# Node degrees from a search in the sorted target list, and a rearranged first third of a graph layer

## The reference

```python
deg = jnp.maximum(jax.ops.segment_sum(jnp.ones(dst.shape), dst, num_segments=6250), 1.0)
xn = _layernorm(x)
f0, f1 = _fctp(x0, x1, W_li0, W_li1, node_attr, MUL)    # f, times 1/sqrt(deg): the gather table
m0, m1 = _fctp(x0, x1, W_lm0, W_lm1, node_attr, MUL)    # m, goes to the residual
# edges: gather f[src], weigh by an MLP of the lengths, segment_sum over dst, times 1/sqrt(deg)
q = elu(xn @ Wq.T) + 1;  k = elu(xn @ Wk.T) + 1;  v = xn @ Wv.T
context = einsum('bhnd,bhne->bhde', k, v);  k_sum = k.sum(axis=2)
x = x + gnn + attention @ Wproj + bproj
x = x + top-2 mixture of 8 experts(layernorm(x))
```

## Time and profile before

| | us |
|---|---|
| median of three runs | 4213.58 |
| the profiled execution, its own time | 4215.28 |
| its span (first to last instruction) | 4213.5 |
| TensorE busy | 4026.7 |
| VectorE, ScalarE, GpSimd busy | 2988.6, 2611.7, 2601.5 |

### The profile page before, as it was taken

How to read it: one execution, slowest core, us unless ns; L and a number is a source line. 1 busy time by engine, 2 the same in 40 slices (tenths; PEclk the granted TensorE clock), 3 DMA queues, 4 the chain that set the end, 5 groups by cost and what they waited for, 6 DMA issues and landing times. The chain is left out here.

```text
span 4213.5 us, 84731 instructions
## 1 busy us (share of the span) xinstructions
PE 4026.7 (96%) x19450; PEld 3335.2 (79%) x19450; DVE 2988.6 (71%) x5419; ACT 2611.7 (62%) x8831; POOL 2601.5 (62%) x2378
## 2 busy tenths in 40 slices
PE   4999599999999999999999999999998689999999
PEld 2888488878888888878887888878798678888887
DVE  6666599999999999999999999999956811010010
ACT  1444488878887788878887788878723423333332
POOL 3444477777777777777777777777611334434433
PEclk8999799999999999999999999999998699999999
DMA  3333333333333333333333333333323146666665
GB/s 120 103 99 104 111 104 103 104 104 103 104 103 104 103 104 104 104 104 103 104 104 103 103 104 104 104 104 103 89 80 108 61 155 189 198 189 194 198 185 158
DMA packets 432355, 497.65 MB, mean 118 GB/s; under 512 B 253143, under 2 KB 343995, under 8 KB 417995
## 3 DMA queue, kind: packets, MB, share of 16 engines
q0 software_dynamic: 105984, 260.17, 21.9%
q1 hardware_dynamic: 326347, 237.18, 19.4%
HBM read 433.72 MB, written 63.33 MB: 118 GB/s over the span
## 5 line engine op out<-in xcount | busy, mean ns | idle before, releaser
L615 POOL DMA_INDIRECT k_x<-gather_table,edges_src x1760 | 1998.4, 1135 | 574.6 <-issue 474.7
L632 ACT ACTIVATE k_x<-k_x,edges_y 128x64 f32<-128x64 f32 x5280 | 1303.1, 336 | 4.6 <-DMA k_x<-gather_table,edges_src 4.6
L738 PE MATMUL edges_ps_sum<-k_x,edges_hot_y 128*128 128x256 f32 x3520 | 1094.1, 392 | 0.5 <-issue 0.5
L738 PE MATMUL edges_ps_sum<-k_x,edges_hot 128*128 128x256 f32 x3520 | 1048.0, 379 | 0.0
L639 ACT ACTIVATE edges_hot_y<-edges_hot,edges_y 128x128 f32<-128x128 f32 x1760 | 562.4, 390 | 507.0 <-DVE edges_hot L678 507.0
L727 PE MATMUL edges_ps_edge<-k_w_e,edges_hT 100*128 100x256 f32 x3520 | 836.4, 380 | 7.9 <-ACT edges_hT L625 7.9
L694 DVE TENSOR_TENSOR k_x<-k_x,edges_ps_edge 128x768 f32<-128x768 f32 x880 | 794.3, 941 | 0.0
L738 PEld LDWEIGHTS edges_ps_sum<-k_x,edges_hot_y 128*128 128x128 f32 x3520 | 633.3, 190 | 175.6 <-issue 107.1
L727 PEld LDWEIGHTS edges_ps_edge<-k_w_e,edges_hT 100*128 100x128 f32 x3520 | 670.5, 191 | 101.9 <-issue 7.6
L738 PEld LDWEIGHTS edges_ps_sum<-k_x,edges_hot 128*128 128x128 f32 x3520 | 669.7, 190 | 91.4
L1343 DVE TENSOR_TENSOR experts_raw<-experts_ps_y,experts_b 128x256 f32<-128x256 f32 x112 | 42.3, 419 | 727.1 <-PE experts_ps_y L1299 727.1
(11 more groups left out here) (233 smaller groups left out, 3976.1 us busy)
## 6 DMA issues: line engine op xcount, KB each, us to landing
experts_w<-in_w SPq DMA_DIRECT2D x112, 1024.0 KB
k_x<-gather_table,edges_src POOLq DMA_INDIRECT x1760
edges_el<-el_hi SPq DMA_DIRECT2D x880, 20.0 KB
edges_el<-el_lo SPq DMA_DIRECT2D x440, 20.0 KB
nodes_el<-in_el SPq DMA_DIRECT2D x46, 170.0 KB, 2.3
el_hi<-nodes_el_hi SPq DMA_DIRECT2D x46, 170.0 KB, 1.9
el_lo<-nodes_el_lo SPq DMA_DIRECT2D x46, 170.0 KB, 2.0
experts_b<-in_b SPq DMA_DIRECT2D x56, 128.0 KB
```

Source lines behind the costliest of these rows:

```text
L615: nc.gpsimd.indirect_dma_start(out=rows[k][:, j, :], out_offset=None, in_=K.table_d.rearrange("t p d -> (t p) d"), in_offset=bass.Indirect ...
L632: x = nc.scalar.activation(Z[k % 2][:, j, MUL * (i + 1):MUL * (i + 2)], rows[k][:, j, 0:MUL], ACT.Identity, scale=y[k][:, j, 1 + i:2 + i])
L738: x = t.matmul(into[:, :, o, :], rows_hot[k % 2][:, j, :], msg[k % 2][:, j, o * D:(o + 1) * D], start=j == 0 and o == 0, stop=j == GC - 1, ...
```

## The change

`setup` and `items` become one block, `prepare`. SP loads first and last target of each row of 512 (`dst_ends`), the last targets of all rows on every partition (`dst_last`, 392 numbers), x in seven pieces, then the weights. The 49 `bn_stats` and `moments` run inside this block, in three parts between the item steps. ScalarE finds for each node how many rows end at or below it, by the sum of `sign(2 node + 1 - 2 last)`, 49 passes.

`nodes` then finds each node's place within one row of 512: GpSimd gathers that row for each of the 128 nodes of a tile by an indirect DMA (`search`, ring of eight buffers), and VectorE counts the targets not above the node (`rank`). Two tiles are searched and ranked in each of the first 25 steps. The degree is the difference of the places of neighbouring nodes, made by two matmuls with a shift matrix in step 27 (`degrees`). The 32 one-hot matmuls and the one-hots are gone. The power is taken in four parts in steps 28 to 31, f of tiles 0 to 31 is scaled and stored in four parts in steps 32 to 35, and from tile 32 on ScalarE scales f as it empties the bank, and SP stores it tile by tile. The min and max parts of elu+1 move from ScalarE to VectorE, with the add for k and one of the residual's two adds; the cast of the lengths moves from VectorE to ScalarE. Keys and values get banks of their own: two for k, one each for v, the transposes and q. After `nodes` the semaphores are cleared, with one barrier more.

```diff
 prepare, VectorE and ScalarE
+            def groups_below(n, k):
+                if not (isinstance(n, int) and n < TC):
+                    act.wait_ge(balanced, n - (TC - 1))
+                nc.scalar.activation(signs[:, k, :], last[:, :], ACT.Sign, scale=-2.0, bias=odd_node[:, bass.ds(n, 1)],
+                                     accum_out=balance[:, bass.ds(n, 1)]).then_inc(balanced, 1)
+            steps(act, NT, TC, TC, groups_below)
...
-            done(v.tensor_reduce(ends[:, 0, :], dst[:, :, :], AX.X, ALU.min))
-            done(v.tensor_reduce(ends[:, 1, :], dst[:, :, :], AX.X, ALU.max))
...
+            norms(0, 2)
             dve.wait_ge(summed, 1)
...
+            norms(2, 35)
             dve.wait_ge(summed, 2)
...
+            norms(35, NT)
...
+            dve.wait_ge(balanced, NT)
+            done(v.tensor_scalar(K.counts[:, 0, 1:], balance[:, :], 0.5, NGR / 2, ALU.mult, ALU.add))
+            done(v.tensor_copy(K.groups_i[:, :], K.counts[:, 0, 1:]))
 nodes, GpSimd
+            def search(n, slot):
+                if not (static(n) and n < RING):
+                    pool.wait_ge(c["ranked"], n - (RING - 1))
+                g.indirect_dma_start(out=dst[slot][:, :], out_offset=None, in_=A["dst_rows"],
+                                     in_offset=bass.IndirectOffsetOnAxis(ap=K.groups_i[:, bass.ds(n, 1)], axis=0),
+                                     bounds_check=NGP - 1, oob_is_err=False).then_inc(dst_in[slot], 16)
+            for n in range(4):
+                search(n, n)
+            g.tensor_tensor(rstd[:, 4:NT], rstd[:, 4:NT], K.minus_half[:, 4:NT], ALU.pow).then_inc(c["rstd"], 1)
...
+                pool.wait_ge(c["b"], n + 1)
                 if old(n):
                     pool.wait_ge(res_out[k], per(n, k) - 16)
-                g.tensor_tensor(res[k][:, :], m_t[k][:, :], tile(x, n), ALU.add).then_inc(c["b"], 1)
-                pool.wait_ge(c["b"], n + 1)
-                g.tensor_tensor(res[k][:, :], res[k][:, :], K.b_proj[:, :], ALU.add).then_inc(c["res"], 1)
+                g.tensor_tensor(res[k][:, :], b_t[k][:, :], K.b_proj[:, :], ALU.add).then_inc(c["res"], 1)
+                if early:
+                    for j in range(2):
+                        if not (static(n) and 2 * n + 4 + j >= NT):
+                            search(2 * n + 4 + j, (2 * k4 + 4 + j) % RING)
 nodes, VectorE
+            def rank(n, slot):
+                dve.wait_ge(dst_in[slot], per(n, slot, 16, RING))
+                if not (static(n) and n < 4):
+                    dve.wait_ge(c["ranked"], n - 3)
+                v.tensor_scalar(passed[:, slot % 4, :], dst[slot][:, :].bitcast(i16).rearrange("p (e h) -> p e h", h=2)[:, :, 0],
+                                K.node[:, bass.ds(n, 1)], None, ALU.is_le, ALU.add,
+                                accum_out=K.counts[:, 1, bass.ds(n + 1, 1)]).then_inc(c["ranked"], 1)
...
+                if static(n) and LATE <= n < LATE + 4:
+                    at = slice((n - LATE) * EIGHT, (n - LATE + 1) * EIGHT)
+                    dve.wait_ge(c["f"], LATE)
+                    v.tensor_tensor(f[:, at, :], f[:, at, :], K.sc_f[:, at].unsqueeze(2).to_broadcast([P, EIGHT, D]),
+                                    ALU.mult).then_inc(c["f_scaled"], 1)
 nodes, TensorE
+            def degrees():
+                pe.wait_ge(c["ranked"], NT)
+                counts = ps_deg.rearrange("p (z t) -> p z t", z=2)
+                t.matmul(counts, K.step[:, 0, :], K.counts[:, :, 1:], start=True, stop=False)
+                t.matmul(counts, K.step[:, 1, :], K.counts[:, :, 0:NT], start=False, stop=True).then_inc(c["deg"], 1)
...
-                for j in range(UC):
-                    z = t.matmul(deg, hot_lo[k][:, :, j], hot_hi[k][:, :, j], start=first and j == 0,
-                                 stop=last and j == UC - 1, skip_group_check=True)
```

More of the change, by code:

```diff
@@ L123, in _ @@
         def _(sp):
+            sp.dma_start(ends[:, :, :].rearrange("p z g -> p (z g)"), A["dst_ends"]).then_inc(ends_in, 16)
+            sp.dma_start(last[:, :], A["dst_last"].to_broadcast([P, NGR])).then_inc(last_in, 16)
+            for h in range(NT // TC):
+                sp.dma_start(K.x2[:, h * TC:(h + 1) * TC, :],
+                             A["x"][h * TC:(h + 1) * TC].rearrange("t p d -> p t d")).then_inc(x_in[h], 16)
             for dst, src in loads:
-                sp.dma_start(dst, src).then_inc(loaded, 16)
-            sp.wait_ge(loaded, 16 * len(loads))
+                sp.dma_start(dst, src).then_inc(weights_in, 16)
+            sp.wait_ge(weights_in, 16 * len(loads))
         @block.gpsimd
@@ L170, in items @@
[L170 to L199, removed]
@@ L421, in _ @@
-            steps(dve, NEL, 2, 2, both)
-            for n in range(NEL, NT):
-                hots(n, n % 2)
-            dve.wait_ge(c["context"], NT)
-            v.tensor_scalar(K.dis[:, :], deg, 1.0, None, ALU.max).then_inc(c["clamped"], 1)
-            dve.wait_ge(c["dis"], 1)
-            v.scalar_tensor_tensor(K.sc_f[:, :], K.dis[:, :], 1 / 80.0, K.attr[:, :], ALU.mult, ALU.mult)
-            v.scalar_tensor_tensor(K.sc_o[:, :], K.dis[:, :], C_X / math.sqrt(128.0), K.attr[:, :],
-                                   ALU.mult, ALU.mult).then_inc(c["scales"], 1)
@@ L457, in turned, with body @@
                     act.wait_ge(c["queries"], n - 1)
-                a.copy(xnT[k][:, :], ps_T[k][:, 0:D]).then_inc(c["xnT"], 1)
-            def emptied(n, k):
+                a.copy(xnT[k][:, :], ps_T[:, 0:D]).then_inc(c["xnT"], 1)
+            def body(n, k4, early):
+                k = k4 % 2
+                if not (static(n) and n + 1 >= NT):
+                    turned(n + 1, 1 - k)
+                if static(n) and n == 2:
+                    act.wait_ge(c["shift"], 2)
+                if not (static(n) and n + 2 >= NT):
+                    normed(n + 2, k)
@@ L461, in emptied @@
                 act.wait_ge(c["fm"], n + 1)
                 pf = ps_f[k][:, :].rearrange("p (c h n) -> p c h n", c=2, h=2)
-                a.copy(tile(f, n).rearrange("p (c n) -> p c n", c=2), pf[:, :, 0, :])
+                if static(n) and n == LATE:
+                    act.wait_ge(c["scales"], 1)
+                if early and not (static(n) and n >= LATE):
+                    a.copy(tile(f, n).rearrange("p (c n) -> p c n", c=2), pf[:, :, 0, :]).then_inc(c["f"], 1)
+                else:
+                    a.activation(tile(f, n).rearrange("p (c n) -> p c n", c=2), pf[:, :, 0, :], ACT.Identity,
+                                 scale=K.sc_f[:, bass.ds(n, 1)]).then_inc(c["f"], 1)
@@ L1388, in program @@
         K.slot_token, K.slot_weight = sb("slot_token", [P, NSLOT // P], i32), sb("slot_weight", [P, NSLOT // P])
-        setup(nc, A, K)
-        items(nc, A, K)
-        nodes(nc, A, K)
+        with ExitStack() as early:
+            first = Mem(nc, early, "first")
+            K.step = first.sb("step", [P, 2, P])
+            K.node, K.groups_i, K.counts = first.sb("node", [P, NT]), first.sb("groups_i", [P, NT], i32), first.sb("counts", [P, 2, NT + 1])
+            K.stats = first.sb("stats", [P, NT, 6])
+            K.mean, K.var, K.diff = (first.sb(z, [P, NT]) for z in ("mean", "var", "diff"))
+            K.moments = first.sem("moments")
+            prepare(nc, A, K)
+            nodes(nc, A, K)
+        nc.clear_and_free_semaphores(nc.allocated_since(unused))
+        nc.all_engine_barrier()
         with ExitStack() as sums:
```

362 lines of the change are left out of this document (208 added, 154 removed).

## The result

The changed kernel took 3994.44 us (median of 4 runs, 3991.1 to 4002.11) beside 4213.71 for the kernel before (4 runs, 4213.45 to 4217.97) on the same chip: ratio 0.948, 95% interval 0.9464 to 0.9496. The execution that was profiled took 3991.1 us with a span of 3989.3.

The account below looks back on a forecast made before the run. TensorE, busy 96% of the span, was taken as the bound. 60 + 114 + 124 + 5 = 303 us to the zero fill against 489.3, 186 less, later stages untouched: 4028 us; range 4000 to 4085, own range 4008 to 4065.

Parts of the forecast that it names:

- Wrong if: Sign passes over 0.7 us, searches over 2, pitch of tiles 36 to 48 above 5.5, edge stage over 5 different.
- Front: Before the tile loop: reordered loads and statistics start the first tile at about 42.5 us, 27 us earlier.
- Entry: From first tile to GpSimd's first q: 17.4 us for searches, powers and adds, so first q at 60.
- Loop, tiles 1 to 22: Tiles with searches: four stations within half a us, 5.2 us a tile (bounds 4.5 and 6.5), 114 us.
- 0.8 over GpSimd's sum: Tiles 1 to 22: allowance for imperfect meshing above GpSimd's 4.4 us, also covering about 1 us of port locks.
- Tiles 23 to 48: Tiles after the searches: TensorE longest, 4.6 us a tile, 5.6 for the four scaling the table; 124 us.
- with clock and loop losses 4.6: Tiles 23 to 48: TensorE's 4.15 us raised to 4.6 a tile, as 0.49 is lost in the old loop.
- Tail: After the loop to the zero fill: last store and boundary 3 us, then 1, semaphore clearing 1; 5 in all.
- clean mesh: Rival for the loop: all stations pack, TensorE sets the pitch; zero fill at 276, 4000 us; chance 0.13.
- Half clock: Rival for the loop: TensorE at 1.2 GHz throughout, 8.3 us a tile, 4187 us; chance 0.04.
- piled-up waits: Rival for the loop: early pitch 6.8, late 5.5 us, zero fill at 361, 4085 us; chance 0.14.
- serialised searches: Rival for the searches: 2 KB-row gathers hold GpSimd over 5.3 us; at 6 us each, 4248 us; chance 0.01.

Follow-up runs that it names:

- one more add: Changed kernel with one more 128x256 add on GpSimd in each of tiles 1 to 22, result unread; pitch 4.89 us by q adds, zero fill 279.55 us.
- the nine runs: Follow-up runs except three with the count or table; changed kernel and variants 4565 to 4682 us, kernel before 4840 to 4936.

## Why the prediction was right, and where it was wrong

As a forecast of the time it missed: 3994.44 us lies below the whole range, 33.6 us from the 4028. The mechanism was right; two terms of the loop were too long, and every error but the tail's points the same way. None of the four signs under "Wrong if" occurred: none of them looks for a loop that is too quick.

Front: right. First tile at 41.30 for 42.5. The sign passes of ScalarE took 0.606 each, as I took; between my bounds of 0.48 and 1.1 that was partly luck. The last ended at 35.0 us, 2.5 before VectorE used the sums.

Entry: right. First q at 57.62 for 60, which is 16.3 us behind the first tile instead of 17.4: six cheaper searches.

Loop, tiles 1 to 22: the step that failed is "They will not mesh perfectly. I take 5.2 us, 0.8 over GpSimd's sum". It measured 4.36, and this is 18.5 of the 34.6 us by which I missed the zero fill. It has two parts. GpSimd's sum was 4.4 in my working, with the search at 1.46; busy time and issue gaps make about 4.0 (0.74 + 0.76 + 2 x 1.25). And the excess was 0.4, not 0.8. The kernel before without its count, at 4.14 with the next station at 86%, shows that queues two buffers deep cost such a loop next to nothing; and with one more add the pitch was GpSimd's sum. Waits of such queues are there, but they mostly fill slack instead of adding up. Of the 0.4, 0.15 is TensorE's 4.15 above GpSimd's sum; the rest is short waits, put down above to the transfers, and which property of them it is stays open. One sign that I named did not come: the granted clock stayed at 1.00 in this stretch.

The rule I leaned on for the 0.8 was that of the Trainium skill, SBUF — State Buffer, section on the two separate sides. It makes the shared ports an exclusive lock, which the instruction that starts first holds to its end. This trace agrees with the rule. Two tiles of the changed kernel, in each VectorE's el_lo (two inputs in SBUF) and GpSimd's q add:

```profile
223.44 0.51 DVE L474 TENSOR_TENSOR nodes_el_lo<-nodes_el,nodes_el_hi 128x340 fp32r<-128x340 f32 x1 [2.34 <-ACT nodes_el_hi L551]
223.68 0.86 POOL L420 TENSOR_TENSOR nodes_q<-nodes_q_high,nodes_q_low 128x256 f32<-128x256 f32 x1 [2.39 <-ACT nodes_q_low L553]
...
250.17 0.73 POOL L420 TENSOR_TENSOR nodes_q<-nodes_q_high,nodes_q_low 128x256 f32<-128x256 f32 x1 [1.14 <-ACT nodes_q_low L553]
250.22 1.04 DVE L474 TENSOR_TENSOR nodes_el_lo<-nodes_el,nodes_el_hi 128x340 fp32r<-128x340 f32 x1
```

Whichever starts second grows with what was left of the first: q by 0.13 us where 0.27 was left, el_lo by 0.53 where 0.68 was. What was wrong is my price, 1 us a tile and all of it on GpSimd. In tiles 1 to 22 el_lo mostly met a search, and then hardly grew (0.50 to 0.58 us), as the search did not (1.00 to 1.02 in 18 of 20 tiles); b met the q add in part of the tiles and waited itself (mean 547 ns there, 418 behind the searches). GpSimd's res add has a mean of 739 ns and its q add 756. In the run with one more add el_lo came beside the two adds, and the one that started behind it took 1.01 us instead of 0.73: hence the res add's mean of 895 ns between 62 and 145 us.

Tiles 23 to 48: 108.9 us for 124, the other 14.7 us (my terms add up to 123.6). The term that failed is "with clock and loop losses 4.6": I carried 0.45 us a tile over from the old loop. The clock loss belonged to the count: it went with it (1.00 here and in the kernel before without its count) and came back with it (0.95). The four tiles with the table took 5.08 instead of 5.6.

Tail: 6.05 for 5. The sum was 303 for a zero fill at 268.45: 2.4 us at the first q, 18.5 and 14.7 in the loop, less 1 here, make the 34.6. Its sign and its mechanism were right; the rival "clean mesh", 276 and 4000 us, was nearer in its numbers and held for 0.13. Half clock, piled-up waits and serialised searches did not occur.

## What to carry to other kernels

When a station that was busy all the time is relieved, start from the next longest sum of busy time and issue gaps and add little: here the waits behind queues two tiles deep added 0 to 0.4 us to 4.1. Before carrying a clock loss over into a forecast, find the stretch of work that has it; if the change takes that stretch out, the loss goes as well. Where two engines hold each other up, as VectorE and GpSimd did here (0.51 or 1.04 us for the same pass), ask which instructions will stand beside each other and which starts first, instead of taking a mean from the old kernel. In a loop where three stations are within a few per cent of each other, no single experiment names "the" bound; relieve one and load another, and read from the trace what the load really cost before you read the slack.

## What the hardware showed that I had not expected

A gather of 128 rows of 2 KB cost GpSimd 1024 ns, less than the 1135 ns of the edge stage's gathers of 1 KB rows: twice the bytes cost GpSimd nothing more.

Counting over a written sum is two instructions on ScalarE, 606 ns and a read of the accumulator of 187 ns, yet the next pass starts 0.6 us after the last: the read is hidden. On VectorE a rank of 512 elements took 737 ns, 54 more than the one-hot of the same width.

On the two chips of the nine runs TensorE did not get its work in the edge stage. This is the groups view of 1000 to 1500 us, in the changed kernel's first profile and in the second:

```profile
L791 PE MATMUL edges_ps_edge<-k_w_e,edges_hT 100*128 100x256 f32 x696 | 164.6, 379 | 0.0
```
```profile
L791 PE MATMUL edges_ps_edge<-k_w_e,edges_hT 100*128 100x256 f32 x544 | 145.3, 414 | 53.2 <-ACT edges_hT L689 51.6 <-issue 1.5
```

In 500 us it did 544 of these instead of 696, waited 53 us, in pauses of up to 8, and had a clock of 0.89. The pauses come to VectorE first, before its add into the accumulators (69.8 us in 14 waits); what holds it there these traces don't say. The whole time of the kernel before grew by 706 us on that chip (4919.86 for 4213.71), that of the changed kernel by 684 (4678.65 for 3994.44), so a difference of 9 us can be read there only in a stretch that is free of such pauses.
